# Attention with a gated output on one core: key tiles 12 and 13 of the last chunk added by GpSimd, normalisation steps at later places, the gate's third token tile loaded beside the last division

## The reference

```python
x = L0_attn_x                                   # (2, 2048, 1024)
xn = _layernorm(x, axis=-1)
# attention: 32 query heads, 8 key/value heads, head size 32, causal
q, k, v = (xn @ wq), (xn @ wk), (xn @ wv)       # k, v repeated for 4 query heads each
scores = where(causal, q k^T * 32 ** -0.5, min)
s = softmax(scores) @ v @ wo
# gate: a linear layer plus the top 2 of 8 low-rank experts, weighed by a router
g = silu(xn @ W_base.T + b_base + 2 * sum_e w_e * (xn @ A_e.T) @ B_e.T)
return x + s * g
```

## Time and profile before

| | us |
|---|---|
| median of 3 runs (3377.36 to 3383.86) | 3378.37 |
| the profiled execution | 3379.06 |
| its span | 3377.3 |
| PE busy | 3274.2 |
| DVE busy | 1880.5 |
| ACT busy | 1439.7 |
| POOL busy | 1355.7 |

### The profile page before, as it was taken

The page is one execution under the profiler, slowest core; times in us unless marked ns, Lnnn a source line. Parts: engine busy times, 40 slices in busy tenths (PEclk is TensorE's granted clock), DMA queues, the critical chain, the costliest instruction groups (busy, mean ns, idle before and its releaser), DMA issues.

```text
span 3377.3 us, 51290 instructions
## 1 busy us (share of the span) xinstructions
PE 3274.2 (97%) x18048; PEld 2195.1 (65%) x18048; DVE 1880.5 (56%) x4622; ACT 1439.7 (43%) x2658; POOL 1355.7 (40%) x549
## 2 busy tenths in 40 slices
PE   6999999799999999999999999999999899999999
PEld 5888888655555555555555555555553688888887
DVE  6333332287777777677777777767773322223333
ACT  3221121046666666566665666666666111111100
POOL 0000000036766766776776676677667000000000
PEclk9999999899999999999999999999999999999999
DMA  6555554345665666656566566656666444445554
GB/s 231 162 156 167 163 174 151 115 98 117 136 139 130 139 133 135 135 126 135 129 136 136 125 143 129 133 131 136 138 154 157 140 151 137 138 153 195 196 191 170
DMA packets 283503, 494.53 MB, mean 146 GB/s; under 512 B 40864, under 2 KB 156576, under 8 KB 263328
## 3 DMA queue, kind: packets, MB, share of 16 engines
q1 hardware_dynamic: 260256, 333.04, 33.0%
q0 software_dynamic: 20736, 151.00, 22.5%
q10 hardware_dynamic: 2304, 7.87, 0.7%
HBM read 205.03 MB, written 134.74 MB: 101 GB/s over the span
## 4 chain that ended last, share of the span: by engine, by line
PE 65%; DMA 6%; DVE 4%; ACT 2%; issue 2%; SPq 1%; POOL 1%; POOLq 0%; ACTq 0%; DVEq 0%
PE o_ps L1295 14%; PE cols_ps L1340 13%; PE rows_ps L1257 12%; PE rows_ps L799 4%; PE rows_ps L800 4%; PE rows_ps L801 4%; PE cols_ps L1313 3%; PE rows_ps L951 3%; PE rows_ps L949 3%; PE rows_ps L950 3%; DVE row_max L1428 2%; DMA l_few<-l_sb 2%; PE cols_ps L1343 1%; DMA l_sb<-scratch_l_inv 1%; DMA scratch_l_inv<-l_few 1%
## 5 line engine op out<-in xcount | busy, mean ns | idle before, releaser
L1223 POOL TENSOR_TENSOR added<-added,probs 128x2048 f32<-128x2048 f32 (+3 forms) x320 | 1169.4, 3654 | 901.8 <-PE o_ps L1295 807.9
L1428 DVE TENSOR_REDUCE row_max<-rows_ps 128x1 f32<-128x512 f32 x1536 | 994.5, 682 | 286.0 <-PE rows_ps L1257 283.2
L1400 ACT ACTIVATE probs<-cols_ps 128x512 f32<-128x512 f32 x1728 | 921.1, 610 | 357.7 <-PE cols_ps L1340 323.7
L1432 DVE CUSTOM_DVE_ANT_0 masked_rows<-rows_ps,tri 128x128 bf16<-128x128 f32 (+3 forms) x1024 | 483.6, 483 | 181.1 <-PE rows_ps L1257 178.2
L1257 PE MATMUL rows_ps<-k_st,q_st 96*128 96x512 f32 (+3 forms) x1536 | 526.9, 371 | 40.4 <-DMA q_st<-scratch_q_hi 17.2
L1340 PE MATMUL cols_ps<-q_st,k_st 97*128 97x512 f32 x1248 | 521.1, 424 | 0.6
L1295 PE MATMUL o_ps<-probs,v_st 128*32 128x512 f32 (+3 forms) x4224 | 441.5, 535 | 0.0
L1340 PE MATMUL cols_ps<-q_st_last,k_st 97*128 97x512 f32 x928 | 381.3, 425 | 5.1 <-ACT dma_added L1400 3.2
L1257 PEld LDWEIGHTS rows_ps<-k_st,q_st 96*128 96x128 f32 x1536 | 296.0, 193 | 136.2 <-DVE row_max L1428 49.2
L1257 PE MATMUL rows_ps<-k_st,q_st_last 96*128 96x512 f32 (+3 forms) x1024 | 366.0, 384 | 2.7 <-DVE row_max L1432 0.2
L1340 PEld LDWEIGHTS cols_ps<-q_st,k_st 97*128 97x128 f32 x1248 | 237.6, 190 | 176.8 <-issue 112.6
(11 more groups left out here) (113 smaller groups left out, 3791.0 us busy)
## 6 DMA issues: line engine op xcount, KB each, us to landing
dma_added<-probs POOLq DMA_DIRECT2D x144, 1024.0 KB, 7.7
q_st<-scratch_q_hi SPq DMA_DIRECT2D x96, 256.0 KB, 5.3
x_sb<-in_x SPq DMA_DIRECT2D x32, 512.0 KB, 4.0
scratch_xt_hi<-xt_hi SPq DMA_DIRECT2D x32, 512.0 KB, 6.0
scratch_xt_lo<-xt_lo SPq DMA_DIRECT2D x32, 512.0 KB, 6.8
scratch_q_hi<-out_hi SPq DMA_DIRECT2D x64, 256.0 KB, 2.5
scratch_q_lo<-out_lo SPq DMA_DIRECT2D x64, 256.0 KB, 2.9
l_sb<-scratch_l_inv SPq DMA_DIRECT2D x256, 64.0 KB, 5.0
```

The lines of the kernel that those rows point to most:

```text
L1223: nc.gpsimd.tensor_tensor(total[:, :, q0:CH], total[:, :, q0:CH], probs_of(c, j)[:, :, q0:CH], ALU.add).then_inc(pool_added, 1)
L1400: nc.scalar.activation(probs_of(c, j)[:, :, i * P:(i + 1) * P], cols_ps[cols_slot(AT_T[t])][:, :].rearrange("p (h q) -> p h q", h=NREP), A ...
L1428: nc.vector.tensor_reduce(into, bank[:, :], AX.X, ALU.max).then_inc(rows_free, 1)
L1432: nc.vector.tensor_tensor_reduce(masked_rows[rows_slot(k)][:, 0:keys], bank[:, 0:keys], tri[:, CH - keys:CH], 1.0, MASKED, ALU.add, ALU.ma ...
```

## The change

Key tiles 12 and 13 of chunk 3 move from `REST` to `ADDS`: POOL adds them and PE's `Y` no longer reads them. The steps I, L2, L3 of every chunk's division stand 4 tiles later, N 3 tiles later and L4 7 tiles later, L1 where it was. The store of the gate's tile 0 and the load of token tile 2 move ahead of the last chunk's `L3`.

```diff
-ADDS = [[0, 1, 2, 3], [0, 3, 5, 6, 7], [0, 3, 5, 6, 8, 9, 10, 11], [0, 3, 5, 6, 8, 10, 11]]
+ADDS = [[0, 1, 2, 3], [0, 3, 5, 6, 7], [0, 3, 5, 6, 8, 9, 10, 11], [0, 3, 5, 6, 8, 10, 11, 12, 13]]
-REST = [[], [], [], [12, 13, 14, 15]]
+REST = [[], [], [], [14, 15]]
     event(_t + 4, "L1", _c)
-    event(_t + 12, "I", _c)
-    event(_t + 13, "L2", _c)
-    event(_t + 17, "L3", _c)
-    event(_t + 23, "N", _c)
-    event(_t + 25, "L4", _c)
+    event(_t + 16, "I", _c)
+    event(_t + 17, "L2", _c)
+    event(_t + 21, "L3", _c)
+    event(_t + 26, "N", _c)
+    event(_t + 32, "L4", _c)
+    def store_first(sp):
+        store(sp, Step(0, 0))
+        wait_apart(sp, acc_full, 2, passed)
+        load(sp, 2, 0)
     def stores_before_last(sp):
-        with sp.Fori(0, NPAIR - 1) as pair:
+        store(sp, Step(0, 1))
+        load(sp, 3, 1)
+        with sp.Fori(1, NPAIR - 1) as pair:
                         elif kind == "L3":
+                            if n.lin(1) == NG:
+                                gate.store_first(sp)
                             wait_apart(sp, l_inv_stored[par], ...)
```

More of the change, by code:

```diff
@@ L825, in products @@
                 tile(pe, Step(pair, u))
-    Gate = namedtuple("Gate", "load_bias load stores_before_last last_stores high tanhs lows first_silu silus first_products "
+    Gate = namedtuple("Gate", "load_bias load store_first stores_before_last last_stores high tanhs lows first_silu silus first_products "
                               "products g_stored")
-    return Gate(load_bias, load, stores_before_last, last_stores, high, tanhs, lows, first_silu, silus, first_products,
+    return Gate(load_bias, load, store_first, stores_before_last, last_stores, high, tanhs, lows, first_silu, silus, first_products,
                 products, g_stored)
```

## The result

The changed kernel takes 3345.16 us (median of 4 runs, 3341.39 to 3346.78) where the kernel before takes 3380.57 us beside it: a ratio of 0.9894, with a 95% interval of 0.9876 to 0.9911. It is 35 us faster. The forecast was 3356 us with a range of 3334 to 3380, so the sign and the range hold, and the gain is more than half as large again as forecast (35 us and 22).

The account below looks back on a forecast made before the run. The prediction took PE, busy 97% of the span, to set the pace. From 3379.1 us profiled, - 24.0 + 21 + 15 - 26.5 - 8 gave 3356.6, so 3356 us at the median, range 3334 to 3380.

Parts of the forecast that it names:

- Part 1: At chunk 3's `Y`, tiles 12 and 13 leave PE: 1.50 us in each of 16 groups, 24.0 us gained.
- Part 2: At chunk 3's `Y`, PE waits for POOL's additions: 15 x 1.4, 21 us lost; bounds 0.4 and 3.6 per group.
- Part 3: Behind the waits at `Y`, PE's clock falls in half of 15 groups at 2 us: 15 us lost.
- The rival without any fall: The clock holds behind the waits at `Y`, so the 15 us loss is zero: 3341 us; chance 0.24.
- Part 4: At chunk 1's division, later steps end DVE's wait at I, PE's wait and the clock fall: 26.5 us gained.
- Part 5: At the gate's start, token tile 2 loads earlier, landing 7.5 us sooner, plus 0.5 of slow clock: 8 us gained.
- covered as I said: In the last group, POOL has 15.3 us before `Y` for 8.3 us of additions, so the wait is covered.
- POOL is late by its worst case everywhere: At chunk 3's `Y`, PE waits 3.6 us and the clock falls 2.7 in every group: 3414 us; chance 0.12.
- The stall only moves: The stall at I moves to another reader of the late data, losing the 26.5 us: 3382 us; chance 0.10.

Follow-up runs that it names:

- my own experiment with N of chunk 2: The whole change, with chunk 2's N and L4 moved behind tile 13's addition on GpSimd: 3444.61 us, ratio 1.0188.
- the one experiment: The whole change, with tiles 12 and 13 of the last group's last chunk back on TensorE: 3338.69 us, ratio 0.9877.
- the other: The change without its two tiles, but with them on GpSimd in the last group only: 3340.51 us, ratio 0.9886.

## Why the forecast was right, and where it was not

The chain of the argument held: a stall at I that goes, a shorter `Y`, a new wait for GpSimd, a load that comes earlier. The total was 11 us too high. The errors of its terms have both signs (-10, +8, -6.7 and -4.5 us, added up below), so it is in part luck that it was not further off.

**Part 1, -24.0 forecast.** Measured: `Y` from 3.98 to 2.50 us, 1.48 x 16 = 23.7. Right.

**Part 2, +21 forecast.** Measured: the distance from the start of the product ahead to `Y`'s start, 0.30 us before, sums in 15 groups to 21.8 us above that. The size is right, and so is the reading that POOL's room is what decides: in 13 of the 15 groups `Y` starts 19.7 us behind the issue of tile 9's DMA, for which POOL had waited for ScalarE, with POOL at work all the time between. In the other two it is not room alone (see the rival below). The waits range from 0.37 to 3.49, as the bounds of 0.4 and 3.6 said.

**Part 3, +15 forecast.** This is a term that was mis-sized. The clock fell behind three of the 15 waits (2.17, 2.32 and 3.21 us), at 1.2 to 1.7 us each within `Y`, 4.6 in all (one of the three slow stretches runs on a little behind its `Y`); not behind half of them at 2. The rival without any fall was closer for this term, 0 against 4.6 where I had 15. The Trainium skill (TensorE: Matmul & The Clock Gate, HAM oscillation), whose rule would have made this term zero, is so nearer than my half; yet the trace does not agree with it as a safe bound: the three falls stand behind shorter waits than the rule names.

**Part 4, -26.5 forecast.** Mis-sized, by its base. The five steps alone gave 33.2 us. The bad groups lost what the earlier trace rows showed; but the good ones, at 117.8, lost half a microsecond as well, which showed only when all ran at 117.25. The least of several paces need not be the pace without the cause. In the trace of before VectorE waited 0.1 to 0.25 us for `l_few` in the groups of 117.8 as well, and PE behind it. The one I had taken for undisturbed has this row at the place:

```profile
1005.51 0.33 PE L1257 MATMUL rows_ps<-k_st,q_st 96*128 96x128 f32 x1 [0.19 <-DVE row_max L1432]
```

Set record by record beside a group with the five steps later, that one comes 0.35 us late and the product behind it another 0.1; nearly all of the difference between the two groups is there.

The cause, the order of L1 and L4 in one queue, was named rightly, and L4 alone shows it.

**Part 5, -8 forecast.** Mis-sized: 12.5 us against the kernel with the later steps, in which this wait had grown from 9.80 to 11.11 us. The forecast had not seen that the steps of part 4 delay this load. Some 2.8 us of the 12.5 only pay that back; against the kernel before, what follows the last `Y` is 10.6 us shorter without the tiles (748.4 and 737.8). The last load went out 10.9 us after `Y`, where I had 12.9 (2641.7 against 2628.84), and landed 5.5 us later, not 6.8. What was left of the wait is 0.45 us, and with it the slow stretch behind it went: the first product takes 0.49 us, not 0.79.

**The last group, covered as I said, was not.** `Y` itself was covered there, as forecast. But the prediction looked only for who waits for POOL, and not at what runs beside it. The row was in the trace: VectorE's split of gate's weights (nine instructions, 11.94 us before, the first of them 2.86 and the rest 1.21) lies just where POOL's additions would now go. The loss is 6.5 us by the one experiment and 5.3 by the other, and that is what is left after the 1.5 that `Y` saves.

**Added up.** Forecast for the 15 groups' tiles: -22.5 + 21 + 15 = +13.5; measured, from the kernel without tiles to the one with 15 groups of them: +3.5. Last group: -1.5 forecast, +6.5 measured. Division: -26.5 and -33.2. Load: -8 and -12.5. Sums: -22.5 and -35.7. The +3.5 is within the noise of its two medians; by the parts above it is -22.2 + 21.8 + 4.6 = +4.2. (The kernel before was 2.2 us slower in the comparison than in the base of the forecast, so 13 us in the sum are 11 in the time.)

The rival "POOL is late by its worst case everywhere" fell as a rule for all groups: the longest wait was 3.49 us, and L3's data came in time in 13 of 15. In the groups of the `Y`s at 1887.24 and 2477.94 its milder form is there: tile 9's DMA waits 0.9 us for tile 7's to land, and N of chunk 2 waits 1.88 and 2.18 us for `l_sb`, more than the 1.58 and 1.88 us that PE then waits at `Y`. So 3.5 of the 21.8 us would hardly be there without the late data. "The stall only moves" fell as well, for the change. It came true in my own experiment with N of chunk 2.

## What to carry to other kernels

An engine that issues DMAs issues them in the order of its list: of every transfer that waits for a slow engine ask what stands behind it, before a step is moved and again after. Work moved to an engine that is idle in the mean should be cut to the room at its place: one tile in 15 groups gained 9.9 us here, where two in the same groups gained nothing as long as the rest of GpSimd's chain stayed as it was. And of a "covered" addition ask not only who waits for it, but which instructions of the neighbour run beside it.

## What the hardware showed that was not expected

**VectorE beside GpSimd.** A VectorE subtraction of 128x1024 with two inputs in SBUF takes 1.21 us alone and 4.2 to 5.9 us beside a GpSimd addition of 128x2048 or 128x1536. GpSimd pays less: tile 12's addition took 5.35 us and tile 13's 4.24 beside the split, where two of tile 12's size take 9.61 together and one of tile 13's takes 3.46 elsewhere.

**The clock behind short waits.** Behind waits of PE of 2.2, 2.3 and 3.2 us the granted clock fell to its lower level; behind others of 3.5, 2.0 and 1.9 us in the same kernel it did not. In the kernel with the last group's tiles on TensorE it fell at two of those three places again and held at the third. With the additions alone it held behind 2.9. No wait at `Y` of under 2.1 us was followed by a fall in any kernel here. Elsewhere shorter ones were: in the kernel before, at chunk 1's division, it fell behind waits of PE of 0.64 us (at 1242.2) and 0.35 us (at 1484.4), each with two of 0.2 to 0.26 us in the 3 us ahead. What decides between equal waits stays open: no run was made for it.

**Two versions at the top.** 3321.4 us (two tiles, N and L4 behind) and 3325.3 us (one tile) ran beside different runs of the kernel before; their ratios, 0.9828 and 0.9837, lie in each other's intervals. Both beat the change; which of them is the better isn't settled.
